# Attention with merged weighted products: 129 columns on TensorE, the low part added by VectorE, row statistics moved behind the normalising

## What is computed

```python
x = x + L0_attn_a(_layernorm(x))   # linear recurrence, gelu, layer norm
x = x + L0_ffn(_layernorm(x))      # softmax scores, top 32 of 256, twice
q = (x @ Wq.T).reshape(b, t, 8, 64)
kv = x @ Wkv_down.T                # 64 columns, shared by all heads
k, v = kv @ Wk_up.T, kv @ Wv_up.T
out = softmax(q k^T / 8) v         # per head, over 1024 keys
x = x + out @ Wo.T                 # (x normalised ahead of it)
x = x + L0_ffn(_layernorm(x))
```

## Time and profile before

| | us |
|---|---|
| median of 3 runs | 1357.16 |
| lowest, highest | 1355.29, 1364.52 |
| profiled execution | 1359.22 |
| its span (first to last instruction) | 1357.5 |
| TensorE, VectorE, ScalarE, GpSimd busy | 1222.2, 1147.6, 1052.3, 954.4 |
| mean granted TensorE clock | 0.974 of 2.4 GHz |

### The profile page before, as it was taken

The page is one execution under the profiler, slowest core; times in us unless marked ns, Lnnn a source line. Parts: engine busy times, 40 slices in busy tenths (PEclk is TensorE's granted clock), DMA queues, the critical chain, the costliest instruction groups (busy, mean ns, idle before and its releaser), DMA issues.

```text
span 1357.5 us, 30767 instructions
## 1 busy us (share of the span) xinstructions
PE 1222.2 (90%) x10252; PEld 751.2 (55%) x10252; DVE 1147.6 (85%) x3124; ACT 1052.3 (78%) x2347; POOL 954.4 (70%) x1098
## 2 busy tenths in 40 slices
PE   5999999688888889999999999999999999677776
PEld 2555554345445546666666666666666666344443
DVE  7999996797999988888777788877878854899998
ACT  3323424786999889999999989999999985877776
POOL 4367553486787777777776777777777773488887
PEclk9999999996999999999999999999999999898988
DMA  6200000100002000010000000000000000000000
GB/s 153 61 1 1 0 0 1 42 1 1 24 28 77 30 20 24 24 25 25 25 25 2 2 2 2 2 2 3 2 2 2 2 2 1 1 31 17 32 17 31
DMA packets 35529, 25.32 MB, mean 19 GB/s; under 512 B 16358, under 2 KB 32044, under 8 KB 35372
## 3 DMA queue, kind: packets, MB, share of 16 engines
q1 hardware_dynamic: 35372, 23.36, 6.1%
HBM read 14.89 MB, written 8.39 MB: 17 GB/s over the span
## 4 chain that ended last, share of the span: by engine, by line
PE 45%; ACT 12%; issue 11%; DVE 9%; POOL 4%; DVEq 0%; DMA 0%; ACTq 0%; POOLq 0%; SPq 0%
PE banks L2123 7%; PE banks L2125 7%; PE banks L2111 6%; PE banks L2064 4%; PE banks L2140 4%; PE banks L2141 4%; DVE arena L1595 4%; PE banks L2142 4%; ACT arena L1218 3%; DVE arena L1590 3%; ACT arena L1230 2%; PE banks L2040 2%; ACT arena L1066 2%; PE banks L2186 1%; PE banks L1987 1%
## 5 line engine op out<-in xcount | busy, mean ns | idle before, releaser
L877 POOL TENSOR_TENSOR arena<-arena 128x512 f16<-128x512 f32 x383 | 437.5, 1161 | 145.1 <-ACT arena L1230 141.3
L1218 ACT ACTIVATE arena<-banks 128x512 f32<-128x512 f32 x512 | 302.6, 599 | 41.8 <-PE banks L2125 37.4
L1674 DVE TENSOR_REDUCE arena<-banks 128x1 f32<-128x512 f32 x512 | 326.3, 680 | 4.8 <-PE banks L2111 2.6
L1230 ACT ACTIVATE arena<-arena 128x512 f16<-128x512 f32 x512 | 315.6, 631 | 0.0
L2140 PE MATMUL banks<-arena 128*128 128x65 f16 x2016 | 211.4, 193 | 1.0
L2141 PE MATMUL banks<-arena 128*128 128x64 f16 x2016 | 211.6, 195 | 0.0
L2142 PE MATMUL banks<-arena 128*128 128x65 f16 x2016 | 210.6, 193 | 0.0
L1700 DVE TENSOR_TENSOR arena<-arena 128x512 f16<-128x512 f32 x129 | 107.5, 834 | 121.4 <-ACT arena L1230 121.2
L1590 DVE MAX8 arena<-arena 128x8 f32<-128x256 f32 x512 | 190.0, 412 | 23.8 <-issue 13.7
L1595 DVE MATCH_REPLACE8 arena<-arena 128x256 f32<-128x256 f32 x512 | 205.7, 409 | 0.9 <-issue 0.4
L2140 PEld LDWEIGHTS banks<-arena 128*128 128x128 f16 x2016 | 187.9, 96 | 31.7 <-issue 9.9
(11 more groups left out here) (241 smaller groups left out, 2591.7 us busy)
## 6 DMA issues: line engine op xcount, KB each, us to landing
arena<-q_store SPq DMA_DIRECT2D x48, 128.0 KB, 2.7
x<-in_L_attn_a_x SPq DMA_DIRECT2D x8, 512.0 KB, 3.9
q_store<-arena SPq DMA_DIRECT2D x32, 128.0 KB, 1.8
out<-x SPq DMA_DIRECT2D x7, 512.0 KB, 2.9
arena<-arena SPq DMA_DIRECT2D x64, 1.0 KB, 1.9
arena<-in_L_attn_a_W_in SPq DMA_DIRECT2D x1, 768.0 KB, 5.8
arena<-in_L_attn_a_W_mid SPq DMA_DIRECT2D x1, 512.0 KB, 7.4
arena<-in_L_attn_a_w_w SPq DMA_DIRECT2D x2, 256.0 KB, 7.7
```

Source lines behind the costliest of these rows:

```text
L877: nc.gpsimd.tensor_tensor(pr_lo[c][:, kt, :], pr[:, kt, :], pr_hi[c][:, kt, :], ALU.subtract).then_inc(a_lP, 1)
L1218: nc.scalar.activation(pr[:, kt, :], ps[6 + kt % 2][:, :], ACT.Exp, scale=SM_SCALE).then_inc(a_P, 1)
L1230: nc.scalar.activation(pr_hi[c][:, kt, :], pr[:, kt, :], ACT.Copy).then_inc(a_hi, 1)
L1674: nc.vector.tensor_reduce(mx_half[c][:, i // 2, i % 2:i % 2 + 1], ps[bank][:, :], X, ALU.max).then_inc(a_mx, 1)
```

## The change

- Items 16 to 62 are "merged": in slices j = 0, 1, 2 of `weighted` the two matmuls with pr_hi become one over all 129 columns of `lat`; the product with pr_lo stays (65 columns). A slice then takes 129 columns of bank 5: output and low part side by side. The fourth slice (j = 3) keeps its three matmuls, since 4 x 129 columns don't fit into the bank's 512. Items 0 to 15 and item 63 stay as they were.
- `normalise` of a merged item first copies the low part of three slices (3 x 64 columns) from PSUM to `o_low`, then takes the reciprocal, adds `o_low` onto the output columns in PSUM, and waits for that before it multiplies.
- In item 0 of batches 2 and 3 the row statistics of the output chunk (`stats_of("out", 2 * B - 3)`) are no longer taken inside `final` but behind `normalise(W - 1)`.
- In the first feed-forward, in tiles 6, 10, 14 and 18, ScalarE does `ffn_sT(t)` ahead of `ffn_exp(t + 1)` in place of behind it.

```diff
+        o_low = carve([TPC - 1, HD])
...
+        def merged(W):
+
+            return ITEMS <= W < ALL - 1
...
                     ffn_zT(f, t + 2, q)
+                    if f == 0 and t in HEAD_STATS_AT:
+                        ffn_sT(f, t, q)
                     ffn_exp(f, t + 1, 1 - q)
-                    ffn_sT(f, t, q)
+                    if f or t not in HEAD_STATS_AT:
+                        ffn_sT(f, t, q)
...
-            def final(J, bank):
+            def final(J, bank, part=(0, 1, 2)):
                 dve.wait_ge(a_fm, J + 1)
                 nc.vector.tensor_tensor(x[:, J, :], x[:, J, :], ps[bank][:, 0:D], ALU.add).then_inc(a_fx, 1)
-                if J % TPC == TPC - 1:
+                if J % TPC == TPC - 1 and part:
                     dve.wait_ge(a_fx, J + 1)
-                    stats_of("out", J // TPC)
+                    stats_of("out", J // TPC, part)
...
+                if merged(W):
+                    o = psum[:, :, :].rearrange("p b c -> p (b c)")[:, 5 * CH:5 * CH + TPC * (1 + 2 * HD)]
+                    o = o.rearrange("p (t d) -> p t d", t=TPC)
                 dve.wait_ge(a_ops, W + 1)
+                if merged(W):
+                    nc.vector.tensor_copy(o_low, o[:, 0:TPC - 1, 1 + HD:]).then_inc(a_O_low, 1)
                 nc.vector.reciprocal(rden, o[:, :, 0]).then_inc(a_O, 1)
                 dve.wait_ge(a_O, W * 2 + 1)
+                if merged(W):
+                    dve.wait_ge(a_O_low, (W - ITEMS) * 2 + 1)
+                    nc.vector.tensor_tensor(o[:, 0:TPC - 1, 1:1 + HD], o[:, 0:TPC - 1, 1:1 + HD], o_low,
+                                            ALU.add).then_inc(a_O_low, 1)
+                    dve.wait_ge(a_O_low, (W - ITEMS) * 2 + 2)
...
-                            final(n, bank)
+                            final(n, bank, () if w == 0 else (0, 1, 2))
...
                 if W:
                     normalise(W - 1)
+                if w == 0 and B > 1:
+                    dve.wait_ge(a_fx, (B - 1) * FINALS)
+                    stats_of("out", 2 * B - 3)
...
-                o = ps[5][:, j * (HD + 1):(j + 1) * (HD + 1)]
+                width = 1 + 2 * HD if merged(W) else 1 + HD
+                o = ps[5][:, j * width:min(CH, (j + 1) * width)]
                 js = slice(j * P, j * P + P)
                 for kt in range(KT):
-                    mm(o, pr_hi[c][:, kt, js], lat[B % 2][:, kt, 0:1 + HD], start=kt == 0, stop=False)
-                    mm(o[:, 1:1 + HD], pr_hi[c][:, kt, js], lat[B % 2][:, kt, 1 + HD:], start=False, stop=False)
-                    last = mm(o, pr_lo[c][:, kt, js], lat[B % 2][:, kt, 0:1 + HD], start=False, stop=kt == KT - 1)
+                    if merged(W) and j < TPC - 1:
+                        mm(o, pr_hi[c][:, kt, js], lat[B % 2][:, kt, :], start=kt == 0, stop=False)
+                    else:
+                        mm(o[:, 0:1 + HD], pr_hi[c][:, kt, js], lat[B % 2][:, kt, 0:1 + HD], start=kt == 0, stop=False)
+                        mm(o[:, 1:1 + HD], pr_hi[c][:, kt, js], lat[B % 2][:, kt, 1 + HD:], start=False, stop=False)
+                    last = mm(o[:, 0:1 + HD], pr_lo[c][:, kt, js], lat[B % 2][:, kt, 0:1 + HD], start=False,
+                              stop=kt == KT - 1)
```

More of the change, by code:

```diff
@@ L345, in hybrid_block_kernel @@
         a_hi = sem("a_exp_high")
+        a_O_low = sem("a_out_low_part")
         a_lD = sem("a_exp_low_dve")
```

## The result

The changed kernel takes **1364.64 us** (median of 20 runs, 1362.87 to 1368.03) against 1356.17 (20 runs, 1353.67 to 1364.52) for the kernel before, on one chip: ratio **1.0061 [1.0050, 1.0072]**. I had forecast 1352.3 and a range of 1346 to 1361. The loss is 8.5 us, outside the range and of the other sign; it is less than the 1% that I took for noise, but the runs tell it apart clearly.

A forecast was written before the change was run, and what follows sets the result against it. TensorE was taken to bound the heavy attention items (432.1 of 441.2 us busy). Terms -4.6 + 2.0 + 0 - 5.0 + 2.7 = -4.9 us, from 1357.16 to 1352.3 us; own range 1348 to 1356.5, wider 1346 to 1361.

The forecast's parts named there:

- Merged products, -4.6 and +2.0: Attention items 16 to 62: shorter TensorE slices give -4.6 us (0 to -8), VectorE's longer normalising +2.0 (0 to +8).
- VectorE, 0.68 us an item: Normalising of merged items: low-part copy and addition into PSUM together take 0.68 us more (bounds 0.45 and 1.4).
- the five below 0.68 us: Merged attention items with slack ahead of TensorE's fourth maximum under 0.68 us; shortfalls add up to 1.8 us.
- with a fourth maximum behind them: 44 merged attention items whose slack was measured between VectorE's first reduction and TensorE's fourth maximum, which waits for it.
- Late row statistics, 0: Batches 2 and 3, item 0: statistics moved behind the last item's normalising only shift TensorE's wait, 0 us (-1 to +0.5).
- If the fall does not come, I give back 6.05 less 1.0: First feed-forward, tile 6: early eviction shortens TensorE's idle place and avoids the half clock from 311 to 332 us, -5.0 us.
- the 2.1 us: The profiled execution's excess over the median of the runs, subtracted to move the forecast from 1354.3 to 1352.3 us.
- the clock falls anyway: Rival: the clock still falls in tile 6 or elsewhere in that stretch, the 5.0 is missing, 1357.3 us; chance 22%.
- Tiles 14, 18 and 10, +2.7: First feed-forward: ScalarE stands for TensorE's transposes, +1.2 us each in tiles 14 and 18, +0.3 in 10 (0 to +4).
- the slower rival, early eviction starving TensorE: Rival, tiles 14 and 18: ScalarE's standing idles TensorE and the clock falls at both, 5.0 us each, 1362 us; chance 15%.

The follow-up runs named there:

- second profile of the kernel before: The kernel before, unchanged, profiled once more: that execution took 1353.04 us; median 1352.98 us, ratio 0.9993.
- the run with tile 6 alone: The kernel before with ScalarE's eviction of transposed sparse rows ahead of the exponentials in first feed-forward tile 6 only: 1358.29 us, ratio 1.0013.
- tiles 14 and 18 alone: The kernel before with ScalarE's eviction of transposed sparse rows ahead of the exponentials in first feed-forward tiles 14 and 18 only: 1362.63 us, ratio 1.0038.
- order alone: The kernel before with only the early ScalarE eviction in first feed-forward tiles 6, 10, 14 and 18: 1364.13 us, ratio 1.0075.
- three copies: The changed kernel with the ScalarE order taken back and two more low-part copies on VectorE in each merged normalising: 1362.21 us, ratio 1.0055 against the kernel before.
- merged products alone: The kernel before with merged products and VectorE's addition only, statistics and ScalarE order as before: 1358.71 us, ratio 1.0027.
- the one without the order: The changed kernel with the ScalarE order of the first feed-forward taken back: 1355.65 us, ratio 1.0002 against the kernel before.

## Why the prediction was wrong

**Merged products, -4.6 and +2.0: right in the mechanism, both too large, and right in their sum partly by luck.** The distances are 57 and 29 ns against 56 and 31. A slice saves 0.04 us (0.70 for 0.74), an item 0.11, not 0.15: typical heavy items go from 10.29 to 10.18 us. Of the 41 heavy items 20 gain this 0.1, 16 gain 0.02 to 0.08 (I had counted on ten that something else than TensorE holds), and five gain nothing or lose. All gains of attention together are 3.3 us, forecast 4.6; all losses 1.1, forecast 2.0 (item 20 0.62, items 59 and 60 0.15 each). So attention from item 1 to the last score is 2.3 us shorter (618.37 against 620.66), forecast -2.6.

**VectorE, 0.68 us an item: right** (0.66 measured), and so was reading the price from slack, item by item: two copies more cost 3.7 us in attention, six items carrying it. Not each short slack is paid, though: of the five below 0.68 us three turn up as longer items. Left out was the place where no slack exists: item 62, whose normalising stands in VectorE's queue ahead of the last one (+0.7). I had counted 44 items "with a fourth maximum behind them" and had not asked what follows the last three.

**Late row statistics, 0: wrong in what they were compared with.** I held the moved work against the waits of the kernel before. With the merged products in place and the statistics early the stand is 2.44 us, the clock falls as it ends, and the move saves 2.5 us of attention.

**"If the fall does not come, I give back 6.05 less 1.0", -5.0: wrong twice. This is the step that failed.** First, the length of the fall changes from execution to execution. Over the nine profiles with the old order in tile 6 a fall begins at 310 to 313 us in eight: 6.8 us long in four, 10.2 in one, 20.5 to 23.9 in three. In the second profile of the kernel before it is 6.8 us long and costs 0.5 at most, since VectorE sets the pace in tiles 6 to 8. The price was about right for an execution with the long fall (5.8 us at tile 11), but not for the median. The profiled execution lay over the median for this very reason, and I subtracted the 2.1 us as if they were noise spread over the kernel. Second, TensorE was not the engine that was late. Freed of the half clock it waits 3.04 us for GpSimd in tile 7, behind VectorE's search, and the clock falls there, over denser work (shown by the run with tile 6 alone). The rival "the clock falls anyway" named this, but priced it at zero gain; beside an execution with the short fall it is a loss of 3.6 us at tile 10, and by the runs with tile 6 alone a ratio of 1.0013.

**Tiles 14, 18 and 10, +2.7: right for 14 and 18 in their direct price, wrong for tile 10, and short of the falls that follow.** The two 1.2 us are measured (1.16 at tile 17, 2.37 in sum at tile 21). Falls of the clock add the rest: 4.1 us at tile 24 for tiles 14 and 18, 9.1 for all four tiles. Tile 10 was put at +0.3 and has no run of its own. With the order edit in all four tiles tile 14's search is 5.5 us late, with tile 6's alone 3.6; of the difference some 1.7 us arise between the searches of tiles 10 and 14, where TensorE stands 2.22 us for GpSimd and the clock falls at 348.3: it went there as in tile 6. So the slower rival, early eviction starving TensorE, is what happened; that the stands bring the falls is read from their order in time and not shown by itself: with the order edit in all four tiles each fall starts within 0.6 us of a stand's end, with tiles 14 and 18 alone it comes 7.9 us behind one. The stated range of up to 1361 stopped short of this rival's own 1362. That 1362 was near the result is luck, for its parts were others: falls of 3.4 us at one or two places, not of 5.0 us at both, and tiles 6 and 10 besides.

**Sum.** Beside the second profile of the kernel before, -5.0 became +3.6 at tile 10, and the rest of the first feed-forward about +5.5 instead of +2.7: together 9.1 us. The medians say 8.8 (order alone). With the order taken back the kernel is at 1.0002, where the working of attention without the first feed-forward would have given -2.6. Of that 0.7 are item 62, and about 1.1 lie behind the second feed-forward: the time from the last search to the end is 9.3 to 9.5 us in five of the six kernels with merged products and 8.0 to 8.5 in the others. In the five a fall of the clock of 11.8 to 18.1 us lies over the last tile, in the others shorter ones. Why it lasts longer in these is open: attention ends over 220 us before. The sixth, with three copies, has 8.12, so merging alone doesn't make it.

Open as well: why the fall at 310 lasts 6.8 us in one execution and 23.9 in the next, with the same instructions and TensorE busy nearly all the time. No experiment separated that. It is not the only place that changes so: in the second feed-forward the falls between 1154 and 1181 us add up to anything from 3.4 to 20.5 us, and from the last normalising to the last search it took 228.3 us in one profile and 232.3 in another.

## What to carry to other kernels

A stand of one engine is worth removing only if that engine is the late one when the stand is over: look at who is busy without a pause in the stretch behind it (here VectorE, 6.00 of 6.00 us), and ask what the freed engine will wait for next. Profile the kernel before more than once ahead of pricing a fall of the clock; if its length differs between executions, it is the spread and not a gain. And price added work by the slack behind it, place by place, the last item included.

## What the runs showed of the hardware that was not expected

- The same program has a fall of TensorE's granted clock at 310 us that lasts 6.8 us (1353.04 us in all) or 23.9 us (1359.22): one stretch explains the 6.2 us between two executions of one kernel.
- A stretch at half clock can be nearly free. With TensorE busy 6.00 of 6.00 us at 0.50, VectorE's next two searches started at 313.36 and 319.63, with tile 6's edit and a clock of 1.00 at 313.35 and 319.17.
- Stands of TensorE that ended at 347.77 (2.22 us, order alone), 317.59 (3.04, changed kernel) and 799.48 (2.44, merged products alone) had a fall of the clock within 0.6 us of their end. Shorter ones are no rule: the stand of 2.14 us ahead of the output projection had a fall in the changed kernel and none in the one without the order; the stand of 1.7 us in tile 6, with the old order there, had a fall within 0.9 us in eight profiles of nine, and none in the one with three copies (310.02); one of 1.41 had a fall (371.68, order alone), one of 1.42 none (366.12, tiles 14 and 18 alone).
- VectorE adds 128x192 fp32 values onto PSUM in 0.37 us, with the next operation 0.40 after its start: hardly dearer than reading PSUM alone (copy of the same size 0.35). Behind the copy the next operation starts after 0.26; behind the addition it waits for the result.
